# Attention scores from two float32r parts instead of three bf16 parts, in one product per head

## The reference

```python
h = _layernorm(x) * (1 + ca) + sa
qkv = (h @ qkv_w + qkv_b)                     # 16 heads of 16, q and k rotated
scores = einsum('bhqd,bhkd->bhqk', q, k) * 16 ** -0.5
scores = where(causal_mask, -inf, scores)
attn = softmax(scores)
x = x + ga * ((attn @ v) @ out_w + out_b)
h = _layernorm(x) * (1 + cb) + sb
x = x + gb * ffn(h)                           # routing: top 2 of 4 groups, top 4 of 16 experts
```

## Time and profile before

| | |
|---|---|
| median of 3 runs | 3247.66 us (3235.09 to 3250.77) |
| profiled execution: span | 3061.1 us, from its first to its last instruction |
| median less span | 186.6 us |
| PE, DVE, ACT, POOL busy | 93%, 73%, 58%, 41% of the span |
| granted TensorE clock, mean | 0.978 of full |

### The profile page before, as it was taken

How to read it: one execution, slowest core, us unless ns; L and a number is a source line. 1 busy time by engine, 2 the same in 40 slices (tenths; PEclk the granted TensorE clock), 3 DMA queues, 4 the chain that set the end, 5 groups by cost and what they waited for, 6 DMA issues and landing times.

```text
span 3061.1 us, 61038 instructions
## 1 busy us (share of the span) xinstructions
PE 2843.4 (93%) x22500; PEld 1573.9 (51%) x22500; DVE 2242.9 (73%) x5047; ACT 1779.3 (58%) x2736; POOL 1253.7 (41%) x1557
## 2 busy tenths in 40 slices
PE   7888799999999999989999999987999999999997
PEld 4433333333433334433333333323888999999997
DVE  7888788888888888899998888822393225566477
ACT  2422466666566665656665566665556666666533
POOL 6766311213521114521114765554305753443176
PEclk9999899999999999999999999998999999999998
DMA  4854323313312322412323535245336765665486
GB/s 163 209 142 106 110 56 65 66 42 76 101 39 56 66 63 59 109 43 37 66 63 91 141 94 123 89 129 152 117 93 204 233 202 175 187 183 173 136 238 193
DMA packets 290690, 359.05 MB, mean 117 GB/s; under 512 B 65404, under 2 KB 243212, under 8 KB 290140
## 3 DMA queue, kind: packets, MB, share of 16 engines
q1 hardware_dynamic: 259516, 279.94, 33.8%
q0 software_dynamic: 26112, 71.34, 7.7%
q10 hardware_dynamic: 4768, 3.88, 0.5%
HBM read 206.25 MB, written 139.21 MB: 113 GB/s over the span
## 4 chain that ended last, share of the span: by engine, by line
PE 49%; ACT 13%; DVE 10%; POOL 7%; issue 7%; DMA 2%; ACTq 1%; POOLq 0%; SPq 0%; DVEq 0%
ACT P L1643 13%; PE PB L1165 10%; PE PB L1092 8%; PE PB L1181 7%; DVE mx L1460 6%; PE PB L1062 6%; PE PB L1039 6%; PE PB L1075 5%; POOL x_slots L1846 4%; PE PB L1106 2%; PE PB L1150 2%; ACTq L1652 1%; POOL yg L1859 1%; PE PB L1129 1%; POOL x_slots L1838 1%
## 5 line engine op out<-in xcount | busy, mean ns | idle before, releaser
L1460 DVE TENSOR_REDUCE mx<-PB 128x1 f32<-128x512 f32 (+3 forms) x2560 | 1406.9, 603 | 214.6 <-PE PB L1039 135.6
L1643 ACT ACTIVATE P<-PB 128x1024 f32<-128x1024 f32 (+3 forms) x1280 | 1095.4, 894 | 643.3 <-PE PB L1075 629.3
L1039 PE MATMUL PB<-KO,QO 64*128 64x512 bf16 (+3 forms) x2560 | 762.0, 353 | 61.5 <-DVE mx L1460 51.5
L1092 PE MATMUL PB<-P,V 128*17 128x512 f32 (+3 forms) x5120 | 599.2, 540 | 11.8 <-POOL P L1797 11.7
L1062 PE MATMUL PB<-QO,KO 64*128 64x512 bf16 (+3 forms) x2560 | 546.8, 353 | 60.0 <-ACT P L1643 33.0
L1039 PEld LDWEIGHTS PB<-KO,QO 64*128 64x128 bf16 x2560 | 203.5, 94 | 718.0 <-DVE mx L1460 533.0
L1075 PE MATMUL PB<-QO,KO 34*128 34x512 bf16 (+3 forms) x2560 | 520.0, 351 | 0.6 <-DMA QO<-nh 0.4
L1797 POOL TENSOR_SCALAR_AFFINE_SELECT P<-P 128x256 f32<-128x256 f32 x512 | 208.6, 414 | 678.8 <-ACT P L1643 673.1
L1165 PE MATMUL PB<-xT,ws 128*128 128x128 f32 x3432 | 433.7, 277 | 7.1 <-ACT xT L1726 7.0
L1165 PEld LDWEIGHTS PB<-xT,ws 128*128 128x128 f32 x3432 | 408.2, 193 | 9.7 <-ACT xT L1726 9.7
L1571 DVE TENSOR_TENSOR haT<-sl,PB 64x128 f32<-64x128 f32 x350 | 101.4, 290 | 411.8 <-ACT sl L1735 407.3
(11 more groups left out here) (178 smaller groups left out, 3218.7 us busy)
## 6 DMA issues: line engine op xcount, KB each, us to landing
xq<-x_slots SPq DMA_DIRECT2D x286, 128.0 KB, 2.8
qk_parts<-pt SPq DMA_DIRECT2D x192, 128.0 KB, 2.4
KO<-qk_parts SPq DMA_DIRECT2D x192, 128.0 KB, 4.1
y_slots<-yo SPq DMA_DIRECT2D x191, 128.0 KB
QO<-qk_parts SPq DMA_DIRECT2D x64, 256.0 KB, 3.4
rden<-rden_rows SPq DMA_DIRECT2D x256, 64.0 KB
y_slots<-mx SPq DMA_DIRECT2D x95, 128.0 KB
v_rows<-vst SPq DMA_DIRECT2D x16, 544.0 KB, 4.0
```

What stands on the lines that cost most here:

```text
L1039: mm = pe.matmul(PB[:, bank, 0:n], QO[half, k3, j, 128 * t:128 * t + 128], KO[half, k3, j, 512 * kc:512 * kc + n], start=True, stop=True)
L1092: mm = pe.matmul(PB[32 * j:32 * j + 17, 7, c0:512], V[:, g % 2, kt, 17 * j:17 * j + 17], P[:, pbuf(g, i, j // 2), j % 2, 0:n], start=kt == ...
L1460: dve.tensor_reduce(mx[:, j, t, kc:kc + 1], PB[:, u.bank[item], 0:n], AX.X, ALU.max).then_inc(s["mx"], 1)
L1643: act.activation(P[:, pbuf(g, i, p), :, 0:n], PB[:, 2 * p:2 * p + 2, 0:n], ACT.Exp, scale=0.25).then_inc(s["exp"], 1)
```

## The change

Q and K are split in two parts held as float32, of which the first is written as float32r by ACT; the second is the difference, which POOL computes in one instruction. The third part, the middle rounding and the buffer `pe_` go. The operands QO and KO have half as many head columns of twice the bytes; a head has 50 rows in its half: Q high, Q high, Q low against K high, K low, K high (48 rows), then two rows for the maxima. `max` uses the 48, the new item `s` all 50, and both read the operands as float32r in one product. The mask products stay bf16, `pv` stays float32. Item `lo` is one chunk behind instead of two, group 0 is loaded after chunk 4 instead of 5, and a group takes 8 loads instead of 20.

```diff
-LOADS = [(z, 64 * odd + row, odd, k, n) for odd in (0, 1)
-         for z, row, k, n in ((0, 0, 0, 2), (0, 32, 0, 2), (1, 0, 0, 1), (1, 16, 0, 1), (1, 32, 1, 1), (1, 48, 1, 1))]
-LOADS += [(z, 64 - 64 * odd + row, odd, k, 1) for odd in (0, 1) for z, row, k in ((0, 0, 2), (0, 16, 0), (1, 0, 0), (1, 16, 2))]
+         for z, row, k, n in ((1, 0, HIGH, 2), (0, 16, HIGH, 2), (1, 32, HIGH, 1), (0, 0, HIGH, 1))]
+M_ROW = 48
...
-        if k == 4 and c > 1:
-            o("lo", c - 2)
+        if k == 4 and c > 0:
+            o("lo", c - 1)
...
+        o("s", g, i, 2)
+        o("s", g, i, 3)
+        o("exp", g, i, 1)
+        maxima(at + (quota + 2) // 4)
         if len(pend) == 2:
             values(*pend.pop(0))
-        maxima(at + (quota + 2) // 4)
-        o("sa", g, i, 3)
-        o("sa", g, i, 2)
         maxima(at + quota // 2)
         if ahead:
-            o("sa", *ahead, 0)
-            o("sa", *ahead, 1)
-        o("sb", g, i, 3)
-        o("sb", g, i, 2)
-        o("exp", g, i, 1)
+            o("s", *ahead, 0)
+            o("s", *ahead, 1)
+            o("exp", *ahead, 0)
+        maxima(at + quota // 2 + (quota + 2) // 4)
         if i >= 2:
             pumped(pumps)
-        maxima(at + quota // 2 + (quota + 2) // 4)
-        if ahead:
-            o("sb", *ahead, 0)
-            o("sb", *ahead, 1)
         maxima(at + quota)
-        if ahead:
-            o("exp", *ahead, 0)
...
-    parts_d = scratch("qk_parts", [B, H, 2, 3, HD, T], BF16)
+    parts_d = scratch("qk_parts", [B, H, 2, 2, HD, T])
...
-        nh = A("nh", [32, 2, 2, 128], BF16)
+        nh = A("nh", [64, 2, 128], F32)
...
-        QO = A("QO", [128, 3, 4, T], BF16)
+        QO = A("QO", [128, 3, 2, T], F32)
-        KO = A("KO", [128, 3, 4, T], BF16)
+        KO = A("KO", [128, 3, 2, T], F32)
+        QR, KR = QO[:, :, :, :].bitcast(F32R), KO[:, :, :, :].bitcast(F32R)
...
-                    mm = pe.matmul(PB[:, bank, 0:n], QO[half, k3, j, 128 * t:128 * t + 128], KO[half, k3, j, 512 * kc:512 * kc + n],
-                                   start=True, stop=True)
+                    mm = pe.matmul(PB[:, bank, 0:n], QR[rows, k3, j // 2, 128 * t:128 * t + 128],
+                                   KR[rows, k3, j // 2, 512 * kc:512 * kc + n], start=True, stop=True)
...
-                    pe.matmul(PB[:, j, 0:n], KO[rows, k3, j, 128 * kt:128 * kt + 128], QO[rows, k3, j, q0:q0 + n],
-                              start=True, stop=False).then_inc(s["sa"], 1)
...
+                    pe.matmul(PB[:, j, 0:n], KR[rows, k3, p, 128 * kt:128 * kt + 128], QR[rows, k3, p, q0:q0 + n],
+                              start=True, stop=True).then_inc(s["st"], 1)
...
-                    dve.tensor_tensor(pt[w][:, 2], pe_[:, c % 2], pt[w][:, 1], ALU.subtract).then_inc(s["lo_v"], 1)
...
-                    act.activation(pt[w][:, 0], r[:, :, :], ACT.Copy).then_inc(s["p_hi"], 1)
-                elif name == "lo":
-                    (c,) = at
-                    q.wait_ge(s["p_rest"], c + 1)
-                    act.activation(pt[c % PT_][:, 1], pe_[:, c % 2], ACT.Copy).then_inc(s["p_mid"], 1)
+                    if c == PT_ - 1:
+                        q.wait_ge(s["m_gate"], 1)
+                        q.wait_ge(s["w_mod"], 16)
+                    act.activation(pt[w][:, HIGH].bitcast(F32R), r[:, :, :], ACT.Copy).then_inc(s["p_hi"], 1)
...
-                    pool.tensor_tensor(pe_[:, c % 2], r[:, :, :], pt[c % PT_][:, 0], ALU.subtract).then_inc(s["p_rest"], 1)
-                elif name == "lo" and not (at[0] < OWN or at[0] > 13):
-                    (c,) = at
-                    w = c % PT_
-                    q.wait_ge(s["p_mid"], c + 1)
-                    pool.tensor_tensor(pt[w][:, 2], pe_[:, c % 2], pt[w][:, 1], ALU.subtract).then_inc(s["lo_g"], 1)
+                    pool.tensor_tensor(pt[c % PT_][:, LOW], r[:, :, :], pt[c % PT_][:, HIGH], ALU.subtract).then_inc(s["p_low"], 1)
```

More of the change, by code:

```diff
@@ L11 @@
 BF16 = mybir.dt.bfloat16
+F32R = mybir.dt.float32r
 ALU = mybir.AluOpType
@@ L223, in plan @@
     o("hi", 15)
-    o("lo", 14)
     o("lo", 15)
@@ L542, in A_ @@
             return pool(name, shape, dt)
-        pt = [A_(f"pt{w}", [128, 3, 4, 512], BF16, late_pools if w < 2 else pools) for w in range(PT_)]
-        ta = A_("ta", [128, 2, 512], F32, late_pools)
-        tb = A_("tb", [128, 2, 512], F32, late_pools)
+        pt = [A_(f"pt{w}", [128, 2, 4, 512], F32, late_pools) for w in range(PT_ - 1)]
+        pt_at = next(p.at for p in pools if p.at + 16384 <= p.end)
+        pt.append(A_(f"pt{PT_ - 1}", [128, 2, 4, 512], F32))
+        ta = A_("ta", [128, 2, 512], F32)
+        tb = A_("tb", [128, 2, 512], F32)
         r_at = next(p.at for p in pools if p.at + 8192 <= p.end)
         r = A_("r", [128, 4, 512], F32)
-        pe_at = next(p.at for p in pools if p.at + 16384 <= p.end)
-        pe_ = A_("pe_", [128, 2, 4, 512], F32)
-        wm_s = nc.alloc_sbuf_tensor_at("wm_s", [128, 2, 1536], F32, offset=pe_at)
-        graw = nc.alloc_sbuf_tensor_at("graw", [4, 4, 256], F32, offset=pe_at + 12288)
+        wm_s = nc.alloc_sbuf_tensor_at("wm_s", [128, 2, 1536], F32, offset=pt_at)
+        graw = nc.alloc_sbuf_tensor_at("graw", [4, 4, 256], F32, offset=pt_at + 12288)
         gneg = nc.alloc_sbuf_tensor_at("gneg", [4, 2, 256], F32, offset=r_at)
@@ L789, in _ @@
                     sync.dma_start(mod_d.rearrange("n b d -> b n d"), graw[:, :, :]).then_inc(s["w_mod"], 16)
+                    q.wait_ge(s["c_p"], 3)
+                    for k in (0, 2):
+                        for odd in (0, 64):
+                            sync.dma_start(KO[odd + M_ROW:odd + M_ROW + 2, k], KO[odd + 32:odd + 34, 2]).then_inc(s["l_one"], 16)
                 elif name == "vstore":
@@ L797, in _ @@
                     w, b, tok = c % PT_, c // 4, (c % 4) * 512
-                    q.wait_ge(*lo_done[c])
+                    q.wait_ge(s["p_low"], c + 1)
                     for z in (0, 1):
-                        for k in range(3):
+                        for k in (HIGH, LOW):
                             for half in (0, 1):
@@ L837, in _ @@
                     q.wait_ge(s["vb"], 32)
-                    for k in (0, 1):
-                        sync.dma_start(KO[96:98, k, 0:4:2, :], KO[96:98, 2, 0:4:2, :]).then_inc(s["l_att"], 16)
-                        sync.dma_start(KO[32:34, k, 1:4:2, :], KO[32:34, 2, 1:4:2, :]).then_inc(s["l_att"], 16)
+                    for odd in (0, 64):
+                        row = odd + M_ROW
+                        sync.dma_start(KO[row:row + 2, 1], KO[row:row + 2, 2]).then_inc(s["l_att"], 16)
                     sync.dma_start(gw_s[:, :, :], gw.rearrange("(k p) n -> p k n", p=128)).then_inc(s["l_att"], 16)
@@ L1649, in _ @@
                     for j in (0, 1):
-                        for k in (0, 1):
-                            row = (96, 32)[j] + k
-                            act.dma_start(QO[row:row + 1, k3, 2 * p + j, :].rearrange("o (t q) -> o t q", q=128),
-                                          nh[16 * j:16 * j + 16, p, k, :]).then_inc(s[f"w_nm{p}"], 16)
+                        for k in (HIGH, LOW):
+                            row = 64 * j + M_ROW + k
+                            act.dma_start(QO[row:row + 1, k3, p, :].rearrange("o (t q) -> o t q", q=128),
+                                          nh[32 * k + 16 * j:32 * k + 16 * j + 16, p, :]).then_inc(s[f"w_nm{p}"], 16)
                 elif name == "oc":
@@ L1741, in _ @@
             q.wait_ge(s["c_p"], 1)
-            pool.memset(KO[96:98, 2, 0:4:2, :], 1.0).then_inc(s["c_p"], 1)
-            pool.memset(KO[32:34, 2, 1:4:2, :], 1.0).then_inc(s["c_p"], 1)
+            for odd in (0, 64):
+                pool.memset(KO[odd + 32:odd + 34, 2], 1.0).then_inc(s["c_p"], 1)
             q.wait_ge(s["c_p"], 3)
```

76 lines of the change are left out of this document (24 added, 52 removed).

## The result

The changed kernel is slower: 3427.02 us median (3415.82 to 3431.27, 4 runs) beside 3241.38 (3231.15 to 3250.77, 4 runs) for the kernel before on the same chip, ratio 1.056 [1.053, 1.060] (in brackets a 95% interval). I had forecast 3089.

The account below looks back on a forecast made before the run. Attention was taken as bound by a loop through ACT and PE (2.67 us a step), afterwards by DVE. Terms -116 - 27 - 16 = -159 take 3061.1 to 2902; with 186.6 carried over, 3089 us, range 3010 to 3235.

Parts of the forecast that it names:

- the cover of DVE's wait: Attention with maxima: two reductions (1.24 us) lie ready during PE's weighted sum (0.98); otherwise DVE idles some tenths a step.
- the 143 us forecast for the two attention stretches: Gain forecast for attention: -116 us with row maxima (343 to 2009) and -27 without them (2009 to 2126).
- 6% on its 2.3 is 0.14, just covered: Attention: a lower granted clock adds 0.14 us to PE's step of 2.3, still under DVE's 2.45.
- rival 2: Attention: float32r weight loads aren't hidden, PE's step is 2.64 us and PE the bound; about 3168 us, chance 0.12.
- The ends of my range: Whole kernel: 3010 to 3235 us, from near the case of DVE never waiting to past unhidden weight loads.
- near the bf16 end: Attention: a float32r product is one pass, priced close to bf16's 0.225 us a pair, taken as 0.25.
- rivals 1 and 3: Paired products: halves don't overlap, 3315 us, chance 0.12; or float32r takes four passes, about 4430 us, chance 0.04.
- First stage, -16: Projections up to the first exponential: -10 us in the first chunks, -6 at the end; ends -25 and +11.
- the chunks with maxima: Projection stage, later chunks: PE and DVE wait for each other, removed work is ACT's and POOL's; gain nothing.
- Tail, -27: Attention without maxima (2009 to 2126): ACT's 75 us of work becomes the bound, 90 us for 117.
- Experts, 0: The experts' stage, after attention up to 3061 us: unchanged, 0.
- 186.6 more, which I carry over unchanged: Whole kernel: the median of 3247.66 us exceeds the profiled span of 3061.1; the difference was added to the forecast.

Follow-up runs that it names:

- e4: The changed kernel run again unmodified, in a quick set: 1.062 of the kernel before, span 3256.5 us.
- e2: The changed kernel with two bf16 parts in place of float32r (16 bits of Q and K): 0.981 of the kernel before.
- e5: The changed kernel with only the maximum products in bf16, score products still float32r: 1.009 of the kernel before.
- e6: The changed kernel with only the score products in bf16, maximum products still float32r: 1.050 of the kernel before.
- e11: The changed kernel with the weighted sum put ahead of each step's first maximum: 1.177 of the kernel before.
- e0: The kernel before, unchanged, run and profiled again in a quick set: 3059.4 us, span 3057.7.
- e3: The changed kernel with the maximum products of groups 1 to 15 issued twice: 1.098 of the kernel before.
- e13: The kernel before with its second score products cut to 64 columns, the rest left out: 0.982 of the kernel before.
- e8: The changed kernel with maximum products in bf16 and half of them issued twice: 1.005 of the kernel before.
- e1: The kernel before, three bf16 parts kept, with only the changed kernel's order of products and sum: 1.019 of the kernel before.
- e12: The changed kernel with two bf16 parts and half of its maximum products issued twice: 0.981 of the kernel before.
- e15: The changed kernel with two bf16 parts and the old order of sum and products: 0.980 of the kernel before.

## Why the prediction was wrong

1. **"In front of it stands its ring of three banks: two reductions (1.24 us) lie ready while PE does the weighted sum (0.98), so that cover holds."** This is the step that failed: the cover of DVE's wait. I asked whether DVE has work during the sum, and it has. I didn't follow the ring round: the product that refills it waits for a reduction that couldn't start before the sum's end, and the next sum starts only 0.42 us behind that product (1004.84 and 1005.26). The loop is 2.68 us (chain of e4); e2 and e5 shorten it, e6 leaves it and e11 lengthens it, each within 0.1 us of what its links say. I had priced "if it fails, DVE idles for some tenths a step": 0.20 a step it is. In the 461 steps that the clock left alone e4 takes 1273 us for e0's 1276: of the 143 us forecast for the two attention stretches almost nothing came, the clock aside.
2. **"6% on its 2.3 is 0.14, just covered"** (the clock, in rival 2). The size and the kind were wrong. The clock doesn't sink evenly by 6%, it halves for about 20 us at a time, and then PE's step is 4.13 us, which nothing covers. It costs 193 us, the whole measured loss. The ends of my range had no such case, though the forecast left PE with slack and rows 1 showed 0.93 in the tail and the first stage, where PE has gaps. So the first step that failed took the gain away, and this one made the loss.
3. **A product "near the bf16 end", 0.25 a pair.** One pass is right, and rivals 1 and 3 are dead: halves do overlap, and there are 2560 records a line. But a 512-wide product lands after 0.50 us where bf16's takes 0.39, and its load is 0.21 on average. The pair's interval hardly matters; the 0.11 of landing does, twice, since it is in the loop (0.44 + 0.50 for 0.33 + 0.39). That is the 0.21 between e4's step and e2's. A latency that I had no term for was worth more than the throughput that I priced.
4. **First stage, -16.** It was +12 (first exponential at 355 for 343). The part forecast for the first chunks came: their period is 12.7 us for 14.3, and the rounding that stood at 146.43 in e0 stands at 135.80 in e4. What was put at nothing, the chunks with maxima, lost it again. ACT's rounding of the ninth and of the last chunk of e4:

```profile
162.01 1.91 ACT L1601 ACTIVATE pt<-r 128x2048 fp32r<-128x2048 f32 x1 [1.22 <-POOL r L1738]
...
346.17 1.91 ACT L1601 ACTIVATE pt<-r 128x2048 fp32r<-128x2048 f32 x1 [1.49 <-POOL r L1738]
```

That is 26.3 us a chunk for seven chunks, where e0 takes 23.7 (163.00 to 328.80) and e5 and e2, with the maxima in bf16, 24.5 and 24.6. The maxima go round a ring of two banks there, but the clock is lower too (0.85 from 150 to 320 us for 0.93 in e0 and 0.90 in e5), and no run tells the longer product from the clock. e2's first exponential is at 330, 11 us before e5's; that lead stands already at the ninth rounding (149.76 and 161.05), and e2 stores half the bytes.
5. **Tail, -27.** It gave -15 (117 to 102). The clock is 0.87 there for 0.94; that this took the rest isn't shown.
6. **Experts, 0.** Right: 936.7 and 934.5.
7. **"The median ... is 186.6 more, which I carry over unchanged."** The number was right by chance for that set and wrong as a reason, since it is no part of the kernel's account.

Rival 2 was the nearest in spirit (a load not hidden, a lower clock) and forecast 3168. Every rival with a chance kept the DVE or PE throughput as bound; none was a loop.

**What stays open:** why the clock falls. Time in which PE stands doesn't order it: over the attention PE is idle for 95 us in e0 (half-clock time 45), 89 in e4 (603), 49 in e3 (261), 149 in e2 (203), 137 in e13 (77). Nor do gaps of 2 us alone. Of the 31 falls in e4's attention 8 begin within 7 us of a gap of 1.5 us or more, and 8 others have no gap over 0.7 us there; in e0 all four such gaps are followed by a fall as well, but none of its eight lasts over 7 us, and the median in e4 is 20. So what differs is less that the clock falls than how often and for how long. More products go with less half-clock time in three pairs (e4 and e3, e5 and e8, e2 and e1) and hardly in a fourth (e2 and e12), and the exposed wait of the ring with more (e11). But e13 has as few full products as e2 and a step nearly as short, and 77 us for its 203; and float32r with the same order has two to three times bf16's. Whether that is its longer product, its weight loads or the type itself no run tells apart. A ring of four banks, which should loosen the loop, wasn't tried: four banks hold scores, one the sums, three are the ring.

The version that beats both kernels is e2, 0.981 [0.976, 0.986], with fewer bits (16 of Q and K for 24); e15 and e12 are level with it.

## What to carry to other kernels

When a wait is taken away, write down every loop that is left (product, reduction, bank, product, sum) with latencies, not busy times: here the second loop takes 2.47 us with bf16 operands, under the first one's 2.67, and the new type lifted it to 2.68. If a change takes work off a full TensorE, read the granted clock in short windows and set the same steps of both kernels side by side, sorted by clock: that separates what the clock takes from what the change does. Never add the difference between a profiled span and a median to a forecast before knowing that both are from the same set of runs.

## What the runs showed of the hardware

- Float32r at 48 to 50 rows: one record a product, 0.50 us for 512 columns at full clock where bf16 takes 0.39; two products in different halves of the rows still run beside each other; loads of 128 columns 212 ns on average (180 at full clock, at 1004.83 in e4), near float32's (193) and unlike bf16's (94). The Trainium skill ("TensorE: Matmul & The Clock Gate", section "Weight-path perf modes") excepts FP32 from the fast weight load; by this measurement float32r loads no faster than float32.
- Clock of 1.2 GHz for about 20 us at a time in a stage in which PE is busy for 1787.65 of 1865 us (e4), with the same idle time as before (77 and 80 us), and needless products that cut the half-clock time (603 to 261 us in e3, 339 to 169 in e8). Such time costs about 0.35 us for each us (e4 beside e0).
- Sets of runs with one kernel at 3059 to 3063 or at 3224 to 3243 us, one chip among them with both. In the changed kernel the difference sits in the experts: 934.50 us in e4 and this in the slower set, with the same counts of instructions and the same bytes at a lower rate (153 for 180 GB/s):

```profile
2315.00:3414.10 1099.10, 944.75 (x6413) 860.31 (x6414) 494.57 (x1466) 532.93 (x1210) 422.07 (x452) 0.93 0.50 153
```
